# Normalising each chunk of a linear attention one chunk later in program order

## The reference

```python
def step(carry, inp):
    kv_state, k_state = carry
    q_ch, k_ch, v_ch = inp
    qp = relu(einsum('bhtd,hdm->bhtm', q_ch, proj))
    kp = relu(einsum('bhtd,hdm->bhtm', k_ch, proj))
    ctx_hist  = einsum('bhtm,bhmd->bhtd', qp, kv_state)
    norm_hist = einsum('bhtm,bhm->bht', qp, k_state)
    aw = einsum('bhtm,bhsm->bhts', qp, kp) * mask
    ctx_intra  = einsum('bhts,bhsd->bhtd', aw, v_ch)
    norm_intra = aw.sum(-1)
    out = (ctx_hist + ctx_intra) / (norm_hist + norm_intra + DELTA)[..., None]
    new_kv = kv_state + einsum('bhtm,bhtd->bhmd', kp, v_ch)
    new_k  = k_state + kp.sum(2)
    return (new_kv, new_k), out
```

## The kernel before

| tile | words | pages |
|---|---|---|
| `kv32`, `kvbf`, `kst32`, `kstbf` (state in fp32, and its bf16 copy for TensorE) | 14048 to 14258 | 27 |
| `nr_sb` (norm and its reciprocal, two halves) | 14272 to 14784 | 27, 28 |
| `bc_sb` (the reciprocal spread to 64 partitions) | 14784 to 15296 | 28, 29 |
| `kst_sb` (each chunk's sum of keys) | 15296 to 15328 | 29 |

## Time and profile before

### The profile page before, as it was taken

One profiled execution on the slowest core, in us unless ns is written; L12 is line 12 of the kernel. 1 busy time (PEld: TensorE's weight loads), 2 busy tenths in 40 slices (PEclk: granted clock), 3 DMA queues, 4 the chain that ended last, 5 costly groups with the idle time before them and its releaser, 6 DMA issues.

```text
span 5833.3 us, 44492 instructions; the slowest of 8 cores (5815.1 to 5833.3 us)
## 1 busy us (share of the span) xinstructions
PE 3498.8 (60%) x12082; PEld 1241.3 (21%) x12082; DVE 1967.9 (34%) x2911; ACT 1083.6 (19%) x1034; POOL 160.1 (3%) x204
## 2 busy tenths in 40 slices
PE   6534555555546666666666667552565657585857
PEld 2111222222211211111111111111222223232323
DVE  3683444444431324334335334352010111010104
ACT  1021111111101032332333333220101011111110
POOL 0000000000000000000000000000000000000000
PEclk9665555555568765555555555556887878796877
DMA  2011000000000110010110110001122111112021
GB/s 63 2 9 12 6 6 6 6 6 6 1 8 7 12 25 7 11 18 0 18 18 0 18 18 0 14 6 12 18 22 20 20 15 29 18 27 31 13 37 58
DMA packets 178841, 91.40 MB, mean 16 GB/s; under 512 B 135188, under 2 KB 168340, under 8 KB 178580
## 3 DMA queue, kind: packets, MB, share of 16 engines
q0 software_dynamic: 158080, 70.99, 10.0%
q1 hardware_dynamic: 15586, 17.14, 0.9%
q10 hardware_dynamic: 4932, 0.43, 0.1%
HBM read 150.85 MB, written 8.67 MB: 27 GB/s over the span
## 4 chain that ended last, share of the span: by engine, by line
PE 51%; DVE 18%; ACT 11%; DMA 11%; issue 7%; DVEq 1%; POOLq 0%; ACTq 0%; POOL 0%; SPq 0%
PE psA L896 8%; ACT scratch L910 5%; PE psB L930 4%; PE psA L1231 4%; PE psB L1238 4%; DVE scratch L722 4%; DVE scratch L946 3%; DMA scratch<-rel_stack 2%; PE psA L570 2%; PE psB L1173 2%; PE psA L1265 2%; PE psA L1167 2%; PE psB L1265 2%; DMA scratch<-up_w 2%; DMA scratch<-suwT 1%
## 5 line engine op out<-in xcount | busy, mean ns | idle before, releaser
L896 PE MATMUL psA<-big,scratch 64*128 64x512 bf16 x1024 | 496.0, 604 | 302.6 <-ACT scratch L910 294.0
L919 DVE TENSOR_TENSOR scratch<-scratch 128x1024 bf16<-128x1024 bf16 x512 | 353.6, 692 | 868.8 <-ACT scratch L910 868.5
L910 ACT ACTIVATE scratch<-psA 128x1024 bf16<-128x1024 f32 x512 | 497.5, 1020 | 734.3 <-PE psB L930 553.9
L1231 PE MATMUL psA<-xnT,scratch 128*128 128x512 bf16 x1024 | 430.0, 420 | 166.8 <-DMA scratch<-gate_w 110.5
L930 PE MATMUL psB<-scratch 128*68 128x512 bf16 x1024 | 491.5, 634 | 20.5 <-DVE scratch L919 20.2
L1238 PE MATMUL psB<-xnT,scratch 128*128 128x512 bf16 x1024 | 428.3, 418 | 40.9 <-DMA scratch<-up_w 27.8
L1167 PE MATMUL psA<-xnT,scratch 128*128 128x512 bf16 x512 | 214.8, 419 | 259.8 <-DMA scratch<-sgwT 255.9
L724 PE MATMUL psB<-scratch,c_onb 1*64 1x256 bf16 x128 | 49.6, 388 | 477.3 <-DVE scratch L722 477.3
L1249 DVE TENSOR_TENSOR scratch<-scratch 128x2048 bf16<-128x2048 bf16 x32 | 39.2, 1225 | 807.6 <-ACT scratch L1247 807.6
L722 DVE RECIPROCAL scratch<-scratch 1x256 bf16<-1x256 f32 x128 | 222.9, 1741 | 13.9 <-DVE scratch L719 0.9
L1173 PE MATMUL psB<-xnT,scratch 128*128 128x512 bf16 x512 | 212.9, 416 | 17.8 <-DMA scratch<-suwT 15.3
(11 more groups left out here) (241 smaller groups left out, 4164.9 us busy)
## 6 DMA issues: line engine op xcount, KB each, us to landing
scratch<-rel_stack POOLq DMA_DIRECT2D x16, 992.0 KB, 8.1
scratch<-x SPq DMA_DIRECT2D x16, 512.0 KB, 3.5
scratch<-gate_w POOLq DMA_DIRECT2D x16, 512.0 KB, 6.0
scratch<-up_w POOLq DMA_DIRECT2D x16, 512.0 KB, 7.7
scratch<-down_w POOLq DMA_DIRECT2D x16, 512.0 KB, 14.4
y<-scratch SPq DMA_DIRECT2D x16, 512.0 KB, 2.6
scratch<-WqkvT POOLq DMA_DIRECT2D x24, 256.0 KB, 4.3
scratch<-sgwT POOLq DMA_DIRECT2D x16, 256.0 KB, 4.5
```

What stands on the lines that cost most here:

```text
L896: P.op("tensor", lambda eng, kc=kc, sp0=sp0, tb=tb, r0=r0, r1=r1, q0=q0, hp=hp: eng.matmul(psA[:, sp0 + tb * 512: sp0 + (tb + 1) * 512], k ...
L910: P.op("scalar", lambda eng, ab=ab, sp0=sp0: eng.activation(ab.ap(), psA[:, sp0:sp0 + 1024], AF.Exp), reads=[pk(psA, [sp0 // 512, sp0 // 5 ...
L919: P.op("vector", lambda eng, ab=ab, est=est, f0=f0: eng.tensor_mul(ab.ap(), ab.ap(), est.ap()[:, f0:f0 + 1024]), reads=[ab.keys, est.keys] ...
L1231: P.op("tensor", lambda eng, hc=hc, ci=ci, tb=tb, wge=wge: eng.matmul(psA[:, tb * 512:(tb + 1) * 512], wge.ap().rearrange("p (ci hh) -> p ...
```

## The change

The six operations of the normalisation are wrapped in a function that is made in pass `ch` but called in pass `ch + 1`, behind that pass's state update; the last one is called after the loop. So the calls come in this order, where C is a chunk's context and norm matmuls, S its state update and N its normalisation: before, C0 S0 N0 C1 S1 N1 ... C15 N15; after, C0 S0 C1 S1 N0 C2 S2 N1 ... C15 N14 N15. No operation, size, tile, buffer or arena offset is added, removed or changed. The tracker works out the waits from the new order.

```diff
+            pend_norm = None
             for ch in range(NCH):
                 pb = ch % 2
                 cb0 = pb * 512
...
                     P.op("scalar", lambda eng: eng.copy(kstbf_r[:, 0:2], kst32.ap((0, 64))[:, 0:2]),
                          reads=[kst32.keys], writes=[kstbf.keys], tag=f"pf_ksb{hp}_{ch}")
-                nrv = nr_sb.ap((0, 1))[:, pb * 256:pb * 256 + 256]
...
+                def mk_norm(ch=ch, pb=pb, cb0=cb0, nb0=nb0, bb0=bb0, hp=hp):
+                    def emit_norm():
+                        nrv = nr_sb.ap((0, 1))[:, pb * 256:pb * 256 + 256]
+                        nrb = scr_bf[0:1, 2 * nr_sb.off_w + pb * 512: 2 * nr_sb.off_w + pb * 512 + 256]
+                        P.op("vector", lambda eng, nb0=nb0, nrv=nrv: eng.tensor_scalar_add(
+                            nrv, psA[0:1, nb0:nb0 + 256], 1e-6),
+                             reads=[pk(psA, [nb0 // 512])], writes=[nr_sb.keys], tag=f"pf_ne{hp}_{ch}")
+                        P.op("vector", lp(lambda eng, nrv=nrv, nrb=nrb: eng.reciprocal(nrb, nrv)),
+                             reads=[nr_sb.keys], writes=[nr_sb.keys], tag=f"pf_nr{hp}_{ch}")
+                        P.op("tensor", lambda eng, bb0=bb0, nrb=nrb: eng.matmul(
+                            psB[0:64, bb0 + 256:bb0 + 512], ones_bf[0:1, 0:64], nrb,
+                            start=True, stop=True),
+                             reads=[nr_sb.keys, ones_bf], writes=[pk(psB, [bb0 // 512])], tag=f"pf_nb{hp}_{ch}")
+                        P.op("vector", lambda eng, bb0=bb0, pb=pb: eng.tensor_copy(
+                            bc_sb.ap((0, 64))[:, pb * 256:pb * 256 + 256], psB[0:64, bb0 + 256:bb0 + 512]),
+                             reads=[pk(psB, [bb0 // 512])], writes=[bc_sb.keys], tag=f"pf_nbe{hp}_{ch}")
+                        P.op("vector", lambda eng, hp=hp, ch=ch, cb0=cb0, pb=pb: eng.tensor_mul(
+                            big0[0:64, hp, ch * 128:(ch + 1) * 128], psA[0:64, cb0:cb0 + 128],
+                            bc_sb.ap((0, 64))[:, pb * 256:pb * 256 + 128]),
+                             reads=[pk(psA, [cb0 // 512]), bc_sb.keys], writes=[big0], tag=f"pf_o0{hp}_{ch}")
+                        P.op("vector", lambda eng, hp=hp, ch=ch, cb0=cb0, pb=pb: eng.tensor_mul(
+                            big0[64:128, hp, ch * 128:(ch + 1) * 128], psA[0:64, cb0 + 128:cb0 + 256],
+                            bc_sb.ap((0, 64))[:, pb * 256 + 128:pb * 256 + 256]),
+                             reads=[pk(psA, [cb0 // 512]), bc_sb.keys], writes=[big0], tag=f"pf_o1{hp}_{ch}")
+                    return emit_norm
+                if pend_norm is not None:
+                    pend_norm()
+                pend_norm = mk_norm()
+            pend_norm()
         wout_r = Hd["WoutT"].ap().rearrange("(ci p) (co q) -> co p ci q", p=128, q=128)
```

## The result

| | before | after |
|---|---|---|
| median of all runs | 5972.71 us (10 runs) | 6067.10 us (11 runs) |
| ratio, undisturbed runs only | | 1.033 (95% interval 1.0272 to 1.0389): slower |
| span of the profiled core | 5833.3 us (core 6) | 6041.4 us (core 3); median of the cores 6013 us |

In some executions of either kernel (6 of the 10 before, 4 of the 11 after) the cores of one die, sometimes of both, show a lower granted clock and take some per cent longer; the ratio leaves these out, the medians of all runs contain them.

What follows compares the result with a forecast made beforehand. Latency along a ring of waits was taken to bound the chunk loop, no engine being full; 7.42 instead of 5.83 us a pass made 23.1 us a pair, 185 over 8 pairs, and 5873 + 185 = 6058 us, range 6000 to 6216.

Steps and rivals of the forecast that it cites:

- The ring of before: Closed chain of waits per pass: L676 to L705 1.73, to L724 3.78, to next L676 0.32; 5.83 us.
- The reciprocal doesn't leave the ring: L722 writes page 27, shared with the state's copy, so L705 to L724 stays 3.78 us in the loop's wait chain.
- The bank's wait: L676 waits for L735 of chunk n-2 on the same PSUM bank; L724 to L676 grows from 0.32 to 1.91 us.
- The period: Time of one pass of the chunk loop: 7.42 us forecast instead of 5.83, 1.59 more.
- A pair: One pair's loop 23.1 us longer: 20.7 in the middle, less 1.2 at the start, plus 3.6 at the end.
- The sum: 8 pairs x 23.1 us = 185 us more for the whole kernel, 3.2% of the profiled execution.
- The clock: TensorE's granted clock, 0.50 in the loop, costed at nothing; its rise after the loop could shift 12 us either way.
- Rival A: Normalisation overlaps the next pass, DVE's own order bounds: 4.89 us a pass, 112 us less, 5761 us; chance 3%.
- B: Rival: L676 still follows L724 by 0.32 us; a pass stays 5.83 us, 5880 us timed, same; chance 6%.
- C: Rival: TensorE's clock rise after each loop is lost for the whole projection, 154 us more, 6212 us; chance 3%.
- the base: Starting time for the forecast: the lower of the two timed runs shown, 5873 us, to which 185 us were added.

Runs made afterwards that it cites:

- b_page: Kernel before (old order, two banks) with 64 words of padding that move `nr_sb` off the state's page 27; ratio to before 0.9810.
- norm64: `b_page` with the norm computed on 64 partitions at once, so the matmul L724 and copy L728 fall away; ratio to before 0.9612.
- a_page: Kernel after with 64 words of padding, so `nr_sb` no longer shares page 27 with the state; two banks; ratio to before 1.0163.
- a_both: Kernel after with both the 64 words of padding and four PSUM banks for the context; ratio to before 0.9816.
- a_banks4: Kernel after with the context in four PSUM banks instead of two; ratio to before 0.9991.
- d_norm64_b4: `norm64` with the normalisation called one pass later and the context in four PSUM banks; ratio to before 0.9515, repeated 0.9564.
- norm64_wait: `norm64` with TensorE's wait for ScalarE put last instead of ahead of VectorE's, no wait removed; ratio to before 0.9665.
- d_norm64: `norm64` with the normalisation called one pass later, two banks; ratio to before 0.9913.

## Why the prediction was right or wrong

- **The ring of before**: 1.73 + 3.78 + 0.32. Confirmed by taking terms out of it: without the copies on ACT (`b_page`) 4.94, without the way over TensorE too (`norm64`) 4.06.
- **The reciprocal doesn't leave the ring**: right, but page 27 was only one of the reasons. What `a_page` takes out of the ring is ACT's two copies (L723 moves up behind L711); the reciprocal stays in it there, and even in `a_both`.
- **The bank's wait brings L728 to L735 into the ring**: right. It was to be seen 112 times and is; the release was put at 0.16 us and is 0.15; the stretch from the spreading matmul to the next context matmul was put at 1.91 us and is 1.90. `a_banks4` takes back all of the loss by removing this wait alone, and `d_norm64_b4` does so in another ring.
- **The period**: 7.42 forecast, 7.31 measured. The miss is in the terms that I took over unchanged: L677 to L706 is 1.70, not 1.73, and L706 to L727 3.71, not 3.78. Nearly all of the second is the 0.77 us ahead of L722, which were 0.84: in the new order L722 has one wait to look at (ACT), in the old one two (ACT, and TensorE for the norm). It is the same kind of term that `norm64_wait` isolates on TensorE; for DVE it is read from the traces only.
- **A pair**: 23.1 us forecast. Here, first state update to last multiplication, 114.3 - 92.3 = 22.0. **The sum**: 185 us forecast. The stage gives 173.8 + 3.2 = 177, 8 us less, and the period's 13 x 8 x 0.11 = 11 us cover that. Between the two profiled executions the median of the cores grew by 187 us (5827 to 6013); that this meets the forecast rests on 9 us more of rest. They are within what the rest differs by from kernel to kernel (4141 to 4168 us), so I don't assign them. The ratio gives 3.3% of about 5850, some 193 us, and its interval goes from 159 to 228.
- **The clock**: costed at nothing, with 12 us either way. The granted clock in the loop is 0.50 after as before. The rise to 1.00 in the projection behind this pair came 4.6 us after it restarted, with TensorE busy for 4.53 of them, against 3.0 us with 2.89 busy before; that is within the range given.
- **Rival A (the overlap works)** and **B (the bank's wait met early)** both fell: periods of 4.89 and 5.83 were their marks. B is what `a_banks4` has by construction, 5.75 and no change of time. A's 4.89 lies close to the 4.91 of `a_both`, but by luck: A was priced by DVE's own order, while in `a_both` DVE still waits 0.36 us for L694, and A's mark, a context matmul that starts ahead of the reciprocal, is not to be seen there either (L679 at 1108.36 follows L729). **C** fell: the clock did rise.
- **The step that failed is the base**, "the lower of the two plus the sum". The forecast of the change was +185 us, 3.2%, and 3.3% came out. The forecast of the time was 6058 us, and the median is 6067. But I added the sum to the lower of the two runs shown, 5873, while the median of before, which a median of after is set against, is 5952 by those two runs and 5973 by ten. Read against these, 6058 says 1.8% and 1.4% slower, about half of what the argument had found. The two runs shown stood 2.7% apart, nearly as much as the change was to cost, and I used that only to widen the range. No single base mends this: 5973 x 1.032 would be 6164, and the median came out at 6067, 1.6% above 5973, because the two medians mix their runs unequally, as said under the table. What the argument gave was 3.2% between like runs, and this is the form in which it holds. That 6058 lies 9 us from 6067 is luck.

## What to carry to other kernels

Deferring a stage by one pass moves its reads of a rotating buffer right ahead of that buffer's next write: count how many operations old the last reader of a buffer is in the new order, because a rotation of two that was free before can become the tightest wait of the loop. Where a tracker works by pages or banks, list what shares one before reordering; 64 words of padding gave 1.9% here (interval 0.9 to 2.9%), and moving the calls gave 2 us at best. And look for the round trip itself: computing the norm where it is needed took another 114 us off the loops (3.9% less than before, the padding included). With four banks and the deferral it is the fastest kernel of the study, 4.4 and 4.9% less than before in its two measurements; with two banks the deferral loses as much there as anywhere, 170 us.

## What the runs showed of the hardware

- The reciprocal of 64x256 elements takes 1.75 us and that of 1x256 takes 1.74 us; one of 1x1024, in the second layer (L946 of the kernel before), takes 6.55 us. So the time goes by the elements of a partition and not by the number of partitions.
- A TensorE operation with two further semaphore waits that are long met, looked at behind the one that comes last, starts 0.35 us after its release (`norm64`); with the same waits turned round it starts 0.14 us after it (`norm64_wait`).
- From the end of a DVE operation to the start of the TensorE operation that it releases took 0.15 to 0.16 us where that wait is the last one looked at (`after`, `a_page`, `d_norm64`), and from ScalarE 0.14 us (`norm64_wait`).
